# The last block's MLP output products in three rounds instead of two

## The chip, the cores and the metric

The kernel runs on one core of a Trainium2 chip. Its engines work side by side, each through its own instructions in order: PE (TensorE, matrix products), DVE (VectorE), ACT (ScalarE), POOL (GpSimd) and SP (SyncE, which issues all transfers here). They meet only at semaphores. The metric is the device time of one execution in microseconds (us).

## What is computed

For x of 2 x 1024 rows of 2048 numbers, a layer norm is followed by a block with attention and an MLP, and that by a mixture of eight low-rank experts; both are added to x. Three lines of the reference matter here, the MLP with its write, and the expert part that comes last:

```python
mlp_out = jax.nn.silu(gate) * up
hidden_states = rat_write(hidden_states, mlp_out, mlp_wod_w, mlp_wab_w, mlp_wab_b, mlp_du_w, mlp_du_b)
x = x + _L0_ffn_ref(_layernorm(x, axis=-1), L0_ffn_A, L0_ffn_B, L0_ffn_Wr, L0_ffn_br)
```

`rat_write` multiplies the MLP's 2048 hidden values of a row with 632 columns of weights: 512 give `out`, 120 give eight `delta_low` and 112 gate values. A product of `delta_low`, soft-plus and exponentials make a gated update of the row's 2048 hidden numbers from them. All of it is fp32.

## The kernel before

The 2048 rows are 16 tiles of 128 rows, four tiles to a block. The kernel has a projection stage, an attention stage and a mixed stage; the change is in the last one, and there in the fourth block, tiles 12 to 15.

A block has 64 steps on PE. Steps 0 to 31 are the products with the MLP's input weights (L1363). Steps 32 to 63 are the products with its output weights (L1375), in two rounds of 16 steps: the first for tiles 0 and 1 of the block, the second for tiles 2 and 3. Each step takes one of 16 slices of the output weights (128 x 632, `m_wod`, 316 KB) and makes, for each of its two tiles, a product of 512 and one of 120 columns into two banks of PSUM. The weights don't stay on the chip: each round reads all 16 slices again, into a ring of five buffers (NW = 5). SP issues the load for the step five ahead when the step at hand is done.

When a round is over, each of its tiles goes through a write (`w`) and an expert part (`e`), spread over the engines:

- low (L1287 PE, L1418 DVE): the eight `delta_low` are transposed; delta (L1293 PE; L1607 to L1621 ACT; L1423 DVE): their product and the soft-plus
- gates, scale, sum (L1428 to L1471 DVE, L1628 ACT): the gated update; x (L1476 DVE): x is added
- stats (L1502 to L1507 DVE); turn (L1263 PE, L1593 ACT) and down (L1321 PE), each in four quarters: the row is transposed and multiplied with the experts' first factor
- router, weigh (L1512 to L1530 DVE, L1653 ACT), lowT (L1328 PE, L1658 ACT), out (L1333 PE, L1537 DVE) four times, store (SP)

The order of all these is written out by hand. Each step of a block has a place (64 for each block, 1 for each step), each part of a tile stands at a base plus a number, and the list is sorted by place:

```python
W_BASE.update({12: 240, 13: 242, 14: 256, 15: 258})
E_BASE = {**W_BASE, 13: 245.5, 15: 261}
```

Every engine walks this one list and issues its own share, so a part that waits holds up all that stands behind it on its engine. A tile's e part begins 8.5 places behind its base, its store stands at 23. The ring that gives banks to turn, lowT and out has two banks (6 and 7) in the blocks and six after the last step.

Of the kernel before, what the change touches and what calls it, by code (L numbers as in the profile page):

```python
# [11 lines left out]
ALU = mybir.AluOpType  # L12
ACT = mybir.ActivationFunctionType
# [88 lines left out]
def program(nc, x, xT, pos, inv_freq, ident_in, causal_in, spread_in,  # L102
# [3 lines left out]
    with ExitStack() as ctx:  # L106
# [992 lines left out]
        W_BASE = {i: 64 * (i // TB) + 48 + 16 * (i % TB) for i in range(NT - TB)}  # L1099
        W_BASE.update({12: 240, 13: 242, 14: 256, 15: 258})  # L1100
        E_BASE = {**W_BASE, 13: 245.5, 15: 261}
        placed = [(40, ("s", 0, "sum", None))]
        placed += [(64 * blk + step, ("m", blk, step, None)) for blk in range(NBLK) for step in range(64)]
        placed += [(64 * blk - (8.5 - k if blk else .5), ("t", blk, "turn", k)) for blk in range(NBLK) for k in range(RD2 * HCH)]
# [57 lines left out]
        for what, i, part, q in order:  # L1162
# [49 lines left out]
        def used_weights(n):  # L1212
            what, i, k = weights[n]
            if what == "w1":
                sp.wait_ge(write_mm, HCH * i + k + 1)
            elif k < 32:
                sp.wait_ge(mlp_mm, 32 * i + k + 1)
            else:
                sp.wait_ge(wod2_mm, wod2_count(i, (k - 32) // MCH, (k - 32) % MCH))

# [35 lines left out]
        def wait_for_emptied(e, *key):  # L1256
            e.wait_ge(one.sem(key), one.emptied(key))
# [9 lines left out]
        def write_pe(what, i, part, q):  # L1267
# [13 lines left out]
            if part == "low":  # L1281
                if what == "a":
                    wait_for_emptied(pe, what, i, "ab")
                else:
                    wait_for_emptied(pe, "d", i // TB, i % TB // 2, 2 * (i % 2) + 1)
# [68 lines left out]
        def mlp_pe(blk, step):  # L1354
            s = weights_needed("m", blk, step)
            if step < 32:
# [9 lines left out]
                return  # L1366
            q2, k = divmod(step - 32, MCH)
            if k == 0:
                for b in range(4):
                    wait_for_bank(pe, "d", blk, q2, b)  # L1370
# [28 lines left out]
        def write_dve(what, i, part, q):  # L1399
# [43 lines left out]
            if part == "scale":  # L1443
                bs = ab_t[:, DR + 2 * NA:ABW].unsqueeze(1).broadcast_to([P, HS, RH])
                if what == "w":
                    wait_for_emptied(dve, "d", i // TB, i % TB // 2, 2 * (i % 2))
                else:
                    wait_for_emptied(dve, what, i, "out")
# [101 lines left out]
        def mlp_dve(blk, step):  # L1550
            if step < 32:
                g2, mc = UNITS[step]
                if g2 == 1:
                    dve.wait_ge(mlp_mm, 32 * blk + step + 1)
                    wait_for_emptied(dve, "m", blk, step - 2)
                    dve.wait_ge(wod2_mm, 34 * blk)
                    if blk == 0:
# [5 lines left out]
                return  # L1563
            q2, k = divmod(step - 32, MCH)
            if k == MCH - 1:
                for e in range(2):
                    q = 2 * q2 + e
                    dve.wait_ge(wod2_mm, wod2_count(blk, q2, k, e))
                    dve.wait_ge(low_mm, nth("low", "w", (blk - 1) * TB + q) if blk else nth("low", "a", q))
                    V.tensor_tensor(ab2[q][:, :], ps[:, 2 * e + 1, 0:ABW], gates_b[1][:, :],  # L1570
                                    ALU.add).then_inc(emptied[2 * e + 1], 1)

# [22 lines left out]
        def write_act(what, i, part, q):  # L1595
# [8 lines left out]
            if part == "delta":  # L1604
# [64 lines left out]
        def mlp_act(blk, step):  # L1669
            if step < 32:  # L1670
# [235 lines left out]
```

## Time and profile before

| | us |
|---|---|
| median of 3 runs | 1874.6 (1873.32 to 1875.7) |
| the profiled execution's time | 1875.35 |
| its span in the profile | 1873.6 |
| PE busy | 1652.1 (88%) |
| DVE busy | 1171.3 (63%) |
| ACT busy | 794.4 (42%) |
| transfers | 348.69 MB |

The busy shares are means over three stages. The change moves work only in the last 130 us of the span, from the end of the fourth block's first round of output products, and that stretch is to be read by itself. A start in the rows below is in us from the span's start.

### The profile page before, as it was taken

What the parts mean: (1) busy time and instruction counts of PE and PEld (TensorE: products, weight loads), DVE (VectorE), ACT (ScalarE), POOL (GpSimd) and SP (SyncE); (2) the same over time, 40 slices, a digit from 0 to 9 for tenths busy, and PEclk for the clock granted to TensorE, in tenths of its full rate; (3) what the DMA queues carried; (4) which work ended last, traced back from release to release, by engine and by line L of the source; (5) the groups of instructions that cost most, each with busy time, mean ns of one, the idle gap of its engine ahead of it and who ended that gap; (6) DMA issues with size and microseconds to landing.
All of it is one profiled execution on the core that took longest, in us unless ns stands there. A gap on an engine that the chain in (4) does not pass through costs nothing.

```text
span 1873.6 us, 23597 instructions
## 1 busy us (share of the span) xinstructions
PE 1652.1 (88%) x8854; PEld 1141.1 (61%) x8854; DVE 1171.3 (63%) x1873; ACT 794.4 (42%) x1486; POOL 268.7 (14%) x243
## 2 busy tenths in 40 slices
PE   6799998799999956799898999887999998999866
PEld 5565655466666635677565677555677565775544
DVE  6678754688888847344347548547458455555576
ACT  1333235588888725344323444223444322341221
POOL 1235432423340000200002000003000002000000
PEclk7899999899999976699898999998999999999987
DMA  7367568588885152476464665554566544655711
GB/s 298 114 262 254 199 172 238 153 214 238 224 231 125 49 208 90 150 243 215 155 201 155 218 219 199 177 177 149 185 230 212 191 164 148 223 194 172 253 76 68
DMA packets 117221, 348.69 MB, mean 186 GB/s; under 512 B 16226, under 2 KB 33250, under 8 KB 101876
## 3 DMA queue, kind: packets, MB, share of 16 engines
q1 hardware_dynamic: 117108, 347.19, 57.3%
q8 instruction: 70, 1.15, 0.3%
q14 instruction: 43, 0.35, 0.1%
HBM read 271.37 MB, written 75.76 MB: 185 GB/s over the span
## 4 chain that ended last, share of the span: by engine, by line
PE 62%; DVE 22%; ACT 5%; issue 5%; DMA 3%; SPq 2%; POOL 1%; DVEq 0%; ACTq 0%; POOLq 0%
PE ps L1363 15%; PE ps L1375 11%; PE ps L396 4%; PE ps L818 4%; PE ps L1278 4%; PE ps L841 4%; PE ps L805 4%; PE ps L1321 3%; PE ps L1263 3%; PE ps L1306 3%; PE ps L1333 2%; ACT a_p L920 2%; SPq L141 2%; DVE m_A L1436 2%; PE ps L369 2%
## 5 line engine op out<-in xcount | busy, mean ns | idle before, releaser
L1363 PE MATMUL ps<-m_yhi,m_win 128*128 128x512 f32 x1024 | 352.8, 413 | 0.8 <-DMA m_win<-mlp_in_split 0.8
L1375 PE MATMUL ps<-m_wod,m_hT 128*128 128x512 f32 (+1 forms) x1024 | 308.6, 450 | 8.0 <-DVE m_hT L1561 8.0
L1375 PEld LDWEIGHTS ps<-m_wod,m_hT 128*128 128x128 f32 x1024 | 171.8, 199 | 150.1 <-issue 149.7
L1363 PEld LDWEIGHTS ps<-m_yhi,m_win 128*128 128x128 f32 x1024 | 195.4, 191 | 50.1 <-issue 4.9
L862 DVE TENSOR_REDUCE a_negmax<-ps 128x1 f32<-128x640 f32 (+7 forms) x176 | 180.7, 1027 | 63.5 <-PE ps L808 62.7
L920 ACT ACTIVATE a_p<-ps,a_negmax 128x128 f32<-128x128 f32 (+7 forms) x256 | 188.8, 751 | 43.1 <-DVE a_negmax L862 41.0
L1363 PE MATMUL ps<-m_ylo,m_win 128*128 128x512 f32 x512 | 204.0, 398 | 0.0
L818 PE MATMUL ps<-ident,a_p 128*128 128x128 f32 x1152 | 157.9, 276 | 16.1 <-DVE a_pT L875 15.9
L1593 ACT ACTIVATE m_turned<-ps 128x512 f32<-128x512 f32 x128 | 74.1, 593 | 190.2 <-PE ps L1263 190.2
L805 PE MATMUL ps<-a_k,a_q 128*128 128x512 f32 (+3 forms) x384 | 124.5, 403 | 16.6 <-ACT a_p L920 14.7
L818 PEld LDWEIGHTS ps<-ident,a_p 128*128 128x128 f32 x1152 | 123.8, 142 | 18.2 <-DVE a_pT L875 16.8
L1363 PEld LDWEIGHTS ps<-m_ylo,m_win 128*128 128x128 f32 x512 | 98.1, 192 | 24.8 <-issue 4.9
L396 PE MATMUL ps<-p_yT,p_wqkv 128*128 128x512 f32 x256 | 112.3, 593 | 0.0
L1263 PE MATMUL ps<-ident,m_hs 128*128 128x128 f32 x464 | 75.4, 296 | 38.9 <-DVE m_hs L1471 14.0
L1561 DVE TENSOR_TENSOR m_hT<-m_raw,ps 128x512 f32<-128x512 f32 x64 | 43.4, 685 | 106.0 <-PE ps L1363 106.0
L875 DVE COPY a_pT<-ps 128x512 f32<-128x512 f32 (+3 forms) x190 | 108.0, 576 | 0.5
L1708 POOL TENSOR_TENSOR m_scale<-m_scale,mhalf 128x2 f32<-128x2 f32 x16 | 12.4, 774 | 629.3 <-DVE m_scale L1489 629.3
L934 ACT ACTIVATE a_pT<-ps 128x512 f32<-128x512 f32 (+3 forms) x154 | 84.1, 547 | 35.9 <-PE ps L818 35.8
L805 PEld LDWEIGHTS ps<-a_k,a_q 128*128 128x128 f32 x384 | 63.4, 192 | 55.2 <-ACT a_p L920 32.2
L1333 PE MATMUL ps<-e_B,e_lowT 128*128 128x512 f32 x128 | 71.1, 668 | 22.9 <-DVE m_hs L1537 22.2
L1263 PEld LDWEIGHTS ps<-ident,m_hs 128*128 128x128 f32 x464 | 60.1, 155 | 50.5 <-DVE m_hs L1471 15.9
L1679 ACT ACTIVATE m_raw<-ps 128x512 f32<-128x512 f32 x64 | 38.2, 598 | 120.7 <-PE ps L1363 99.0
(202 smaller groups left out, 2737.7 us busy)
## 6 DMA issues: line engine op xcount, KB each, us to landing
m_win<-mlp_in_split SPq DMA_DIRECT2D x128, 512.0 KB, 4.3
m_wod<-in_wod2T SPq DMA_DIRECT2D x128, 316.0 KB, 3.1
m_wod<-in_wod1T SPq DMA_DIRECT2D x64, 316.0 KB, 3.1
p_xT<-in_xT SPq DMA_DIRECT2D x16, 1024.0 KB, 8.9
p_x<-in_x SPq DMA_DIRECT2D x16, 1024.0 KB, 10.4
a_q<-qk_split SPq DMA_DIRECT2D x64, 256.0 KB, 6.5
a_k<-qk_split SPq DMA_DIRECT2D x128, 128.0 KB, 7.1
mlp_in_split<-a_w_two SPq DMA_DIRECT2D x32, 512.0 KB, 3.4
```

The lines of the kernel that those rows point to most:

```text
L396: m = nc.tensor.matmul(ps[:, b, :], wq[:, k, col:col + P], yT[:, k, :], start=(ic == 0), stop=(ic == HCH - 1))
L805: nc.tensor.matmul(ps[:, bank + at, c0:c0 + kn], qs[s][:, qt * P:qt * P + P], ks[s][:, k0:k0 + kn], start=True, stop=k0 + kn < klen)
L818: m = nc.tensor.transpose(ps[:, b, P * m_:P * m_ + P], src[:, j, P * k:P * k + P], ident[:, :])
L841: m = nc.tensor.matmul(ps[32 * hh:32 * hh + 32, 6, c0:P * qn], a_v[s][:, k, HD * hh:HD * hh + HD], kept[:, hh, k, c0:P * qn], start=(k == ...
L862: V.tensor_reduce(negmax[:, n % 4, 0:len(units[n][3])], by_head(n, score_banks(n)), AX_X, ALU.max, negate=True).then_inc(max_ready, 1)
L875: V.tensor_copy(kept[:, heads[j0]:heads[j1] + 1, k0:k1 + 1, P * q:P * q + P], ps[:, b, 0:P * len(part)].rearrange("p (a k b) -> p a k b", ...
L920: m = S.activation(dst[:, j, :], src[:, j, :], ACT.Exp, bias=negmax[:, n % 4, j:j + 1], accum_out=rsum[:, si % 2, q * 4 + hh:q * 4 + hh + 1])
L934: S.activation(kept[:, heads[j0]:heads[j1] + 1, k0:k1 + 1, P * q:P * q + P], ps[:, b, 0:P * len(part)].rearrange("p (a k b) -> p a k b", a ...
L1263: m = nc.tensor.transpose(bank_of(what, i, "turn", q)[:, P * j:P * j + P], h[:, P * (4 * q + j):P * (4 * q + j) + P], ident[:, :])
L1333: nc.tensor.matmul(bank_of("e", i, "out", q), lT[i % 2][:, :], wB[:, 512 * q:512 * q + 512], start=True, stop=True).then_inc(eout_mm, 1)
L1363: m = nc.tensor.matmul(bank_of("m", blk, step), win[s][:, wl, ic, :], y[:, k, :], start=(ic == 0 and p3 == 0), stop=(ic == HCH - 1 and p3 ...
L1375: m = nc.tensor.matmul(ps[:, b, 0:cn], hT[:, k, P * q:P * q + P], w2[s][:, c0:c0 + cn], start=(k == 0), stop=(k == MCH - 1))
```

## The change

In the fourth block the output products go in three rounds: tiles 12 and 13 together as before, then tile 14 alone, then tile 15 alone. The block has 80 steps instead of 64. A step of the two new rounds has two products instead of four, and reads a slice of 316 KB as every step does, so the third reading adds 16 transfers, 5.2 MB.

The parts of tile 14 keep their places (base 256), and those of tile 15 move by 14 for the write (258 to 272) and by 13 for the expert part (261 to 274). Tile 14's banks are 0 and 1 and tile 15's 2 and 3, as before. The ring of banks for the last parts has four (6, 7, 0, 1) after the last step instead of six.

```diff
-        W_BASE.update({12: 240, 13: 242, 14: 256, 15: 258})
-        E_BASE = {**W_BASE, 13: 245.5, 15: 261}
+        W_BASE.update({12: 240, 13: 242, 14: 256, 15: 272})
+        E_BASE = {**W_BASE, 13: 245.5, 15: 274}
+
+        ROUNDS = [[(0, 1), (2, 3)]] * (NBLK - 1) + [[(0, 1), (2,), (3,)]]
...
-        placed += [(64 * blk + step, ("m", blk, step, None)) for blk in range(NBLK) for step in range(64)]
+        placed += [(64 * blk + step, ("m", blk, step, None)) for blk in range(NBLK)
+                   for step in range(32 + MCH * len(ROUNDS[blk]))]
...
-                for b in range(4):
-                    one.plan(("d", i, (part - 32) // MCH, b), b)
-            if what == "m" and (i, part) == (NBLK - 1, 63):
-                one.banks = [6, 7, 0, 1, 2, 3]
+                for q2 in ROUNDS[i][(part - 32) // MCH]:
+                    for b in (2 * (q2 % 2), 2 * (q2 % 2) + 1):
+                        one.plan(("d", i, q2, b % 2), b)
+            if what == "m" and (i, part) == (NBLK - 1, 79):
+                one.banks = [6, 7, 0, 1]
...
-            for e in range(2):
-                q = 2 * q2 + e
-                for c0, cn, b in ((0, H, 2 * e), (H, ABW, 2 * e + 1)):
-                    m = nc.tensor.matmul(ps[:, b, 0:cn], hT[:, k, P * q:P * q + P], w2[s][:, c0:c0 + cn],
-                                         start=(k == 0), stop=(k == MCH - 1))
-                if e == 1 or k == MCH - 1:
+            for q in tiles:
+                for c0, cn, b in ((0, H, 0), (H, ABW, 1)):
+                    m = nc.tensor.matmul(bank_of("d", blk, q, b)[:, 0:cn], hT[:, k, P * q:P * q + P],
+                                         w2[s][:, c0:c0 + cn], start=(k == 0), stop=(k == MCH - 1))
+                if q == tiles[-1] or k == MCH - 1:
                     m.then_inc(wod2_mm, 1)
```

The rest of the diff gives each wait the count that belongs to the new rounds, and lets the copies behind a round go over the round's tiles.

How the list changes the order is seen at two places. The first is PE around the turn of tile 14 (`m_hs_165` is tile 14's hidden row, `e_lowT_200` belongs to tile 13's expert product, `m_wod` to an output product). Before, no output product is left at this point:

```order
L1328 MATMUL ps<-ident,e_weighted_142 128x128
L1333 MATMUL ps<-e_B,e_lowT_200 128x512 x2
L1263 MATMUL ps<-ident,m_hs_165 128x128 x8
L1333 MATMUL ps<-e_B,e_lowT_200 128x512 x2
L1321 MATMUL ps<-e_A,m_turned_188 128x136 x4
L1263 MATMUL ps<-ident,m_hs_165 128x128 x4
```

In the changed kernel the same chain of parts has tile 15's steps between them; shown are steps 9 to 12 of its 16:

```order
L1340 MATMUL ps<-ident,e_weighted_142 128x128
L1388 MATMUL ps<-m_wod_137,m_hT 128x512
L1388 MATMUL ps<-m_wod_137,m_hT 128x120
L1345 MATMUL ps<-e_B,e_lowT_200 128x512
L1388 MATMUL ps<-m_wod_129,m_hT 128x512
L1388 MATMUL ps<-m_wod_129,m_hT 128x120
L1345 MATMUL ps<-e_B,e_lowT_200 128x512
L1275 MATMUL ps<-ident,m_hs_165 128x128 x8
L1388 MATMUL ps<-m_wod_131,m_hT 128x512
L1388 MATMUL ps<-m_wod_131,m_hT 128x120
L1345 MATMUL ps<-e_B,e_lowT_200 128x512 x2
L1388 MATMUL ps<-m_wod_133,m_hT 128x512
```

Seven of tile 15's steps (9 to 15) now stand behind tile 13's weighted values, and five of them (11 to 15) behind the turn of tile 14.

The second place is DVE behind tile 14's sum (the first row of each). Before, tile 15's gates (`m_gate_181`, lane 0) follow at once, and then tile 13's router weights and tile 15's scale:

```order
L1471 TENSOR_TENSOR m_hs_165<-m_hs_165,m_A_168 128x512x3
L1428 TENSOR_TENSOR m_delta_177<-m_delta_177,m_tmp_179 128x512
L1430 SCALAR_TENSOR_TENSOR m_gate_181<-m_mlp_ab_176,m_gate_181 128x48
L1436 TENSOR_TENSOR m_A_167<-m_delta_177,m_gate_181 128x1536
L1437 TENSOR_SCALAR m_gate_181<-m_gate_181 128x48
L1439 RECIPROCAL m_gate_181<-m_gate_181 128x48
L1441 TENSOR_TENSOR m_gate_181<-m_gate_181,m_mlp_ab_176 128x48
L1525 RECIPROCAL e_moments_155<-e_moments_155 128x1
```

In the changed kernel tile 13's router weights, tile 14's x and stats and tile 13's four out additions come first:

```order
L1484 TENSOR_TENSOR m_hs_165<-m_hs_165,m_A_168 128x512x3
L1538 RECIPROCAL e_moments_155<-e_moments_155 128x1
L1540 TENSOR_SCALAR e_router_198<-e_router_198,e_moments_155 128x8
L1543 SCALAR_TENSOR_TENSOR e_weighted_142<-e_low_196,e_moments_155,e_router_198 128x128
L1489 TENSOR_TENSOR m_hs_165<-m_hs_165,m_x 128x2048
L1515 BN_STATS e_stats_152<-m_hs_165 128x6 x4
L1517 BN_AGGR e_moments_156<-e_stats_152 128x2
L1519 TENSOR_SCALAR e_moments_156<-e_moments_156 128x1
L1520 TENSOR_SCALAR e_moments_156<-e_moments_156 128x1
L1550 TENSOR_TENSOR m_last_hs_218<-ps,m_last_hs_218 128x512 x4
L1583 TENSOR_TENSOR m_mlp_ab_176<-ps,m_gate_bias_146 128x120
L1525 SCALAR_TENSOR_TENSOR e_low_150<-e_Asum,e_moments_156,ps 128x136
```

Tile 15's first DVE instruction (L1583, which reads the finished products of its round) moved from ahead of tile 14's gates to behind tile 14's stats.

## Rows read from the trace of the kernel before

**Rows 1.** Busy time of each engine by stretch of 10 us, end of the span
```profile
core 0: us, PE busy (x) PEld busy (x) DVE busy (x) ACT busy (x) POOL busy (x), PEclk, DMA share, GB/s
1770.00:1780.00 10.00, 3.36 (x14) 1.74 (x12) 9.76 (x12) 1.48 (x1) 0.00 (x0) 0.91 0.94 349
...
1820.00:1830.00 10.00, 0.41 (x1) 0.18 (x1) 9.70 (x14) 1.48 (x1) 0.00 (x0) 0.50 0.18 74
```

**Rows 2.** Timeline of PE: start, duration, line, operation [idle before <- releaser]
```profile
1746.21 2.32 PE L1375 MATMUL ps<-m_wod,m_hT 128*128 128x512 f32 x8
1748.37 1.03 PE L1293 MATMUL ps<-m_duT,m_lowT 128*128 128x512 f32 x2
...
1756.79 1.89 PE L1333 MATMUL ps<-e_B,e_lowT 128*128 128x512 f32 x4
...
1781.32 1.97 PE L1263 MATMUL ps<-ident,m_hs 128*128 128x128 f32 x8 [7.96 <-DVE m_hs L1476]
1783.08 5.47 PE L1375 MATMUL ps<-m_wod,m_hT 128*128 128x512 f32 x16
...
1795.45 1.10 PE L1321 MATMUL ps<-e_A,m_turned 128*128 128x136 f32 x8
1796.38 2.32 PE L1375 MATMUL ps<-m_wod,m_hT 128*128 128x512 f32 x8
1798.54 1.10 PE L1321 MATMUL ps<-e_A,m_turned 128*128 128x136 f32 x8
1799.47 1.04 PE L1263 MATMUL ps<-ident,m_last_hs 128*128 128x128 f32 x8
```

**Rows 3.** Timeline of DVE in the same stretch and after it
```profile
1757.85 0.69 DVE L1537 TENSOR_TENSOR m_hs<-ps,m_hs 128x512 f32<-128x512 f32 x1 [1.70 <-PE ps L1333]
...
1773.10 0.68 DVE L1428 TENSOR_TENSOR m_delta<-m_delta,m_tmp 128x512 f32<-128x512 f32 x1
...
1778.98 2.28 DVE L1476 TENSOR_TENSOR m_hs<-m_hs,m_x 128x2048 f32<-128x2048 f32 x1
...
1796.22 0.14 DVE L1507 TENSOR_SCALAR e_moments<-e_moments 128x1 f32<-128x1 f32 x1
...
1809.32 0.68 DVE L1537 TENSOR_TENSOR m_hs<-ps,m_hs 128x512 f32<-128x512 f32 x1
...
1825.23 0.68 DVE L1428 TENSOR_TENSOR m_delta<-m_delta,m_tmp 128x512 f32<-128x512 f32 x1
```

**Rows 4.** Timeline of DVE: weighted values, one tile's statistics, a router
```profile
1828.69 0.16 DVE L1525 RECIPROCAL e_moments<-e_moments 128x1 f32<-128x1 f32 x1
...
1829.45 0.69 DVE L1449 TENSOR_TENSOR m_tmp<-m_delta,m_mlp_ab 128x512 f32<-128x512 f32 x1
...
1841.01 2.46 DVE L1502 BATCH_NORM_STATS2 e_stats<-m_hs 128x6 f32<-128x512 f32 x4
...
1843.94 1.28 DVE L1537 TENSOR_TENSOR m_last_hs<-ps,m_last_hs 128x512 f32<-128x512 f32 x2
...
1851.46 0.34 DVE L1512 SCALAR_TENSOR_TENSOR e_low<-e_Asum,e_moments,ps 128x136 f32<-128x136 f32 x1
...
1853.43 0.35 DVE L1530 SCALAR_TENSOR_TENSOR e_weighted<-e_low,e_moments,e_router 128x128 f32<-128x128 f32 x1
```

**Rows 5.** Timeline of ACT: a soft-plus, first and last instruction
```profile
1749.43 0.60 ACT L1607 ACTIVATE m_tmp<-ps 128x512 f32<-128x512 f32 x1 [4.23 <-PE ps L1293]
...
1751.79 0.24 ACT L1621 ACTIVATE m_gate<-m_gate 128x48 f32<-128x48 f32 x1
```

**Rows 6.** Timeline of PE at the end of the span
```profile
1862.32 0.33 PE L1328 MATMUL ps<-ident,e_weighted 128*128 128x128 f32 x1 [1.71 <-DVE e_weighted L1530]
1863.02 5.40 PE L1333 MATMUL ps<-e_B,e_lowT 128*128 128x512 f32 x8 [0.37 <-ACT e_lowT L1658]
```

**Rows 7.** Issue to landing of the output weights' transfers, 1740 to 1800 us
```profile
DMA to landing us min/median/max: 2.8/3.3/5.5
```

**Rows 8.** Busy time by stretch, a stretch of 2 us
```profile
1720.00:1722.00 2.00, 2.00 (x9) 1.15 (x8) 1.97 (x2) 0.00 (x0) 0.00 (x0) 1.00 1.00 423
```

More of the change, by code:

```diff
@@ L1197, in up_step, with wod2_done @@
             return UNITS.index((1, mc))
-        def wod2_count(blk, q2, k, e=1):
-            return 17 * (2 * blk + q2) + k + 1 + (1 if k == MCH - 1 and e == 1 else 0)
+        wod2_count, wod2_steps = {}, 0
+        for blk in range(NBLK):
+            for r, tiles in enumerate(ROUNDS[blk]):
+                for k in range(MCH):
+                    for q in tiles[-1:] if k < MCH - 1 else tiles:
+                        wod2_steps += 1
+                        wod2_count[blk, r, k, q] = wod2_steps
+        def wod2_done(blk, r, k):
+            return wod2_count[blk, r, k, ROUNDS[blk][r][-1]]
         weights = []
@@ L1218, in used_weights @@
             else:
-                sp.wait_ge(wod2_mm, wod2_count(i, (k - 32) // MCH, (k - 32) % MCH))
+                sp.wait_ge(wod2_mm, wod2_done(i, *divmod(k - 32, MCH)))
         def load_weights(n):
@@ L1284, in write_pe @@
                 else:
-                    wait_for_emptied(pe, "d", i // TB, i % TB // 2, 2 * (i % 2) + 1)
+                    wait_for_emptied(pe, "d", i // TB, i % TB, 1)
                 wait_for_bank(pe, what, i, "low")
@@ L1366, in mlp_pe @@
                 return
-            q2, k = divmod(step - 32, MCH)
+            r, k = divmod(step - 32, MCH)
+            tiles = ROUNDS[blk][r]
             if k == 0:
-                for b in range(4):
-                    wait_for_bank(pe, "d", blk, q2, b)
+                for q in tiles:
+                    wait_for_bank(pe, "d", blk, q, 0)
+                    wait_for_bank(pe, "d", blk, q, 1)
             wait_for_emptied(pe, "m", blk, up_step(k))
-            for e in range(2):
-                q = 2 * q2 + e
-                for c0, cn, b in ((0, H, 2 * e), (H, ABW, 2 * e + 1)):
-                    m = nc.tensor.matmul(ps[:, b, 0:cn], hT[:, k, P * q:P * q + P], w2[s][:, c0:c0 + cn],
-                                         start=(k == 0), stop=(k == MCH - 1))
-                if e == 1 or k == MCH - 1:
+            for q in tiles:
+                for c0, cn, b in ((0, H, 0), (H, ABW, 1)):
+                    m = nc.tensor.matmul(bank_of("d", blk, q, b)[:, 0:cn], hT[:, k, P * q:P * q + P],
+                                         w2[s][:, c0:c0 + cn], start=(k == 0), stop=(k == MCH - 1))
+                if q == tiles[-1] or k == MCH - 1:
                     m.then_inc(wod2_mm, 1)
@@ L1445, in write_dve @@
                 if what == "w":
-                    wait_for_emptied(dve, "d", i // TB, i % TB // 2, 2 * (i % 2))
+                    wait_for_emptied(dve, "d", i // TB, i % TB, 0)
                 else:
@@ L1555, in mlp_dve @@
                     wait_for_emptied(dve, "m", blk, step - 2)
-                    dve.wait_ge(wod2_mm, 34 * blk)
+                    if blk:
+                        dve.wait_ge(wod2_mm, wod2_done(blk - 1, 1, MCH - 1))
                     if blk == 0:
@@ L1563, in mlp_dve @@
                 return
-            q2, k = divmod(step - 32, MCH)
+            r, k = divmod(step - 32, MCH)
             if k == MCH - 1:
-                for e in range(2):
-                    q = 2 * q2 + e
-                    dve.wait_ge(wod2_mm, wod2_count(blk, q2, k, e))
+                for q in ROUNDS[blk][r]:
+                    dve.wait_ge(wod2_mm, wod2_count[blk, r, k, q])
                     dve.wait_ge(low_mm, nth("low", "w", (blk - 1) * TB + q) if blk else nth("low", "a", q))
-                    V.tensor_tensor(ab2[q][:, :], ps[:, 2 * e + 1, 0:ABW], gates_b[1][:, :],
-                                    ALU.add).then_inc(emptied[2 * e + 1], 1)
+                    V.tensor_tensor(ab2[q][:, :], bank_of("d", blk, q, 1)[:, 0:ABW], gates_b[1][:, :],
+                                    ALU.add).then_inc(one.sem(("d", blk, q, 1)), 1)
         def mix_dve():
@@ L1614, in write_act @@
                 else:
-                    wait_for_emptied(act, "d", i // TB, i % TB // 2, 2 * (i % 2) + 1)
+                    wait_for_emptied(act, "d", i // TB, i % TB, 1)
                 act.wait_ge(hs_ready, nth_before("sum", what, i))
@@ L1682, in mlp_act @@
                 return
-            q2, k = divmod(step - 32, MCH)
+            r, k = divmod(step - 32, MCH)
             if k == MCH - 1:
-                for e in range(2):
-                    q = 2 * q2 + e
-                    act.wait_ge(wod2_mm, wod2_count(blk, q2, k, e))
+                for q in ROUNDS[blk][r]:
+                    act.wait_ge(wod2_mm, wod2_count[blk, r, k, q])
                     act.wait_ge(hs_ready, nth("sum", "w", (blk - 1) * TB + q) if blk else nth("sum", "a", q))
-                    S.activation(outs2[q][:, :], ps[:, 2 * e, :], ACT.Copy).then_inc(emptied[2 * e], 1)
+                    S.activation(outs2[q][:, :], bank_of("d", blk, q, 0), ACT.Copy).then_inc(
+                        one.sem(("d", blk, q, 0)), 1)
         def mix_act():
```

## The prediction, made before the changed kernel ran

> **What bounds the kernel now.** I read three views in this order. First the busy time by stretch: in the last 100 us DVE is the full engine, with 9.7 to 9.8 us of 10 in stretches in which PE has 0.4 to 3.4 [rows 1]. So the products are not what sets the end there; DVE's work on one tile's write and expert part is, together with the chain that leads to its start. Second, the timelines of PE and DVE side by side: PE stops 7.96 us for DVE's x of tile 12 before it turns that tile [rows 2], and DVE's tasks stand without a gap from 1757.85 to 1796.36 (38.5 us) and again from 1809.32 on [rows 3]. Between the two DVE has a hole of 13 us, in which PE finishes tiles 14 and 15. That hole, and PE's stop, are what a change of rounds can fill. Third, the end: from the last weighted values, transposed at 1862.32, to the span's end at 1873.6 it is 11.3 us, products, additions and the last store [rows 6].
>
> The change adds no product. It makes tile 14 ready earlier and tile 15 later, and puts steps of tile 15 behind waits for DVE. I therefore follow the new list from about 1744, where the second round begins and up to which the order is the same.
>
> **Part 1, tile 14's first five steps: 5.4 us gained.** A step of two tiles takes 2.16 us (1746.21 to 1748.37) [rows 2], so one of one tile takes 1.08. Ahead of tile 11's out product at 1756.79 [rows 2] stand five steps in both kernels: it moves 5 x 1.08 = 5.4 earlier, to 1751.4, and DVE's addition behind it from 1757.85 to 1752.4. The soft-plus of tile 13 takes 2.6 us on ACT [rows 5] and is over by 1752.9, when DVE still has the addition to do, so nothing else ends late. DVE's block of 38.5 us has the same instructions in the same order [rows 3]: it now ends at 1790.9, and tile 12's x, before at 1781.3, at 1775.9. PE does steps 5 to 10 meanwhile and stops for x from about 1762, 14 us instead of 8.
>
> **Part 2, tile 14 is ready, 7.9 us gained.** After tile 12's turn PE has five steps, downs and turns. By the rows before that took from 1781.32 to 1798.54 [rows 2]; with half the steps and the low clock at its start I get 1775.9 to 1788.2. But DVE takes tile 14's products only behind tile 13's statistics, at 1790.9 to 1791.2. From there PE has to pass, before tile 12's first out addition: low 0.1, four steps of tile 15 (4.3), three downs at 0.93 (1795.45 to 1796.38, so 2.8) [rows 2], delta 0.9 (1.03 long, overlapping what follows) [rows 2], two turns and a lowT (1.0, from 1.04 for two quarters) [rows 2]. That is 9.1, and 1.06 to the addition (1756.79 to 1757.85 [rows 2, 3]): 1801.4, where it was 1809.32 [rows 3].
>
> **Part 3, tile 14's gates to stats.** DVE's block from that addition to tile 14's sum is the same list, 1809.32 to 1825.23, 15.9 us [rows 3]: it ends at 1817.3. Then come tile 13's weighted values (0.8) [rows 4], tile 14's x (2.2) and its statistics, 1841.01 to 1843.94, 2.9 [rows 4]: 1823.2. Up to here the changed kernel is ahead.
>
> **Part 4, tile 15's last seven steps, where the gain is lost.** PE ends step 8 of tile 15 at about 1809.1 and then finds the transpose of tile 13's weighted values in its queue, which come at 1818.1: 9 us of idle PE. Then it has the transpose and its copy (0.4), steps 9 and 10 and two out products (3.9 at the upper clock, some 6.3 with the restart at the lower), two quarters of tile 14's turn, which share two banks with these outs and wait for DVE's additions behind the statistics (1.3), and then steps 11 to 15 (5.4), two outs (1.75), three downs (2.8) and two turns (0.9). Sum: 1818.1 + 0.4 + 6.3 + 1.3 + 10.9 = 1837.0. Before, tile 15's products were complete at 1798.5 [rows 2]; they are 38 us later, and DVE, which has nothing but four additions after 1823.2, waits for them.
>
> **Part 5, tile 15 alone.** From 1837.0: the last down 0.93 (it stands ahead of low), low, router and copy 1.1, delta 0.95, soft-plus 2.6 [rows 5], ACT's copy of tile 14's transposed values 0.3, the out product and its addition 1.06: DVE goes on at 1844.0. One tile's gates, scale and sum with its neighbour's outs took 1757.85 to 1773.10, 15.25 us [rows 3], and x 2.3 [rows 3]: 1861.5. In the kernel before, all of this work of tile 15 was laid between tile 14's, with DVE full [rows 1]. Then PE alone: two quarters turned at the lower clock 1.97 [rows 2], four downs 3.7, two turns 0.9, and about 1.1 for what of the downs falls to the lower clock: 7.7. From the router's first instruction to the end of the weighted values 2.3 (1851.46 to 1853.78) [rows 4], and the 11.3 from there to the end [rows 6]. Sum: 1861.5 + 7.7 + 2.3 + 11.3 = 1882.8.
>
> **The sum.** The span goes from 1873.6 to 1882.8, +9.2. The profiled execution's time is 1875.35, 1.75 above its span and 0.75 above the median of three; I add the 9.2 to the median: 1883.8 us, 0.5% slower.
>
> **Costs with two bounds.** *The clock.* After a stop PE restarts at the lower of its levels: 8 transposes took 1.97 us after the stop of 7.96, and 1.04 without one; two steps of two tiles right behind took 5.47 where one takes 2.32 [rows 2], so 4.5 for two; 1820 to 1830 shows a granted clock of 0.50 (the 1.2 GHz level) with PE idle [rows 1]. I carry 2.4 us for this in part 4, 2.0 in part 5 and 1.8 in the last eight products, whose eight records took 5.40 [rows 6] where four at the upper level took 1.89 [rows 2]. With none of it the sum is 1876.6; with the lower level in part 5's first products too, +1.5, it is 1884.3. The nearest row is the restart at 1781.32, which paid, so I keep the middle value. The Trainium skill says as much (TensorE: Matmul & The Clock Gate, "Loop structure matters more than you think"): products with long waits between them run at the lower clock, which here speaks against the change, since it makes the stop at tile 12 longer and adds one at tile 13. By this rule, the trace agrees.
>
> *The third reading of the weights.* A step needs 316 KB in 1.08 us, 300 GB/s, twice the rate of before. A slice lands 2.8 to 5.5 us after its issue, 3.3 in the middle [rows 7], and five buffers leave four steps, 4.3 us, between the issue and the use. At 3.3 it costs nothing; at 5.5 each step takes 5.5 / 4 = 1.38, 0.3 more. Only steps on the path pay: five in part 1 had their loads issued in the slow first round, four in part 2 while PE stopped, and the five of part 4 too, since their loads are issued by 1819. I take 0, and 1.5 as the upper bound (five steps), nothing below 0, since a transfer can't hasten a step. The engines moved 423 GB/s in a stretch of 2 us [rows 8], so 300 is within reach.
>
> The Trainium skill gives a limit of about 358 GB/s for one core's HBM traffic (DMA: Bandwidth & Descriptors, "Specifications"). The 423 GB/s in a row of this case is above it, so the row decides. By the page a slice would take 0.9 us, an estimate from its figure, still less than a step, and the sum would stay.
>
> *The ring of banks.* Two banks instead of six for the last parts of tile 13 and 14: 0.9 us of the 1.3 above at part 4. The least is 0, the most two DVE additions, 1.4.
>
> **Rivals.**
> *A, the overlap works.* PE gets tile 15's products done while DVE is on tile 14, in the 9 us that it has free, and DVE goes from tile 13's out additions at 1825.7 straight on to tile 15's gates: 1825.7 + 15.25 + 2.3 = 1843.3, + 21.3 = 1864.6, so 1865.6 us, 9 faster. It decides at tile 15's last step: by 1818.7 it is A, later it is not. For it speaks PE's room; against it, the order, which has seven of the steps behind values that come at 1818.1. 6%.
> *B, about the same.* The two gains hold and the clock stays up nearly everywhere: span 1876.6, 1877.6 us. Against it is the restart at 1781.32 [rows 2]. 10%.
> *C, the weights come late as well.* Slices land late beside the 1 MB loads and stores, in part 2 and part 4, some nine steps at 0.3 and one stop of 2 for a slice behind such a store: + 4.7, 1888.5. For it speaks the share of 0.94 at 349 GB/s in 1770 to 1780, when slices and two 1 MB loads go together [rows 1]. 12%.
> *D, the change doesn't do what it says* (the products of tile 14 not complete before those of tile 15): excluded, the new order on PE shows both rounds apart.
> The forecast, 1879.5 to 1886.5, has the other 72%.
>
> **How the numbers follow.** What a measurement of this kernel can tell from no change is about 0.2%, 3.7 us. Faster is A, 6%. Same is B and the lowest edge of the forecast, 10%. Slower is the rest of the forecast and C, 84%. The range leaves out A and the edges of B and C: 1878.0 to 1889.0.
>
> **What would show it.** In the changed kernel's profile: DVE's addition to tile 11's row at about 1752.4 and tile 14's sum ending near 1817 (parts 1 to 3); PE idle some 14 us before 1776 and 9 us before 1818 on DVE's x and weighted values (part 4); tile 15's bias addition (L1583) near 1837; a hole of more than 10 us on DVE between 1829 and 1844; tile 15's x at 1861. If that bias addition comes before 1820, A holds. If PE's waits for slices (on the transfers of the weights) are above 2 us in total, C. If the clock reads 1.0 from 1818 to 1826 and at the last turn, B. What would make the prediction wrong is a wait that I have put in the wrong place in part 4, since each us there goes to the end undiminished.

## The result and the profile after

The changed kernel takes 1884.5 us (median of 4 runs, 1883.8 to 1887.0), the kernel before on the same chip 1875.2 (1873.3 to 1875.8). The ratio is 1.0054, with a 95% interval from 1.0037 to 1.0071: slower by 0.5%. The interval belongs to the record's ratio over all runs; the quotient of the two medians is 1.0050. Forecast were 1883.8 and a range from 1878.0 to 1889.0.

The profiled execution has a span of 1885.2 us, 11.6 more than before. The second round begins 1.0 us later in it (VectorE's addition of the bias for tile 12 at 1742.95, before at 1741.94), and up to there both kernels have the same order, so that microsecond isn't the change's. From this addition to the end it is 142.25 us, before 131.66: **+10.6**. The kernels are compared below by this tail and by their medians. A tail is that of one execution, here the slowest of the four, and the medians differ by 9.4.

The busy page tells little: the sums hardly move (PE 1652.1 to 1658.3 us, DVE 1171.3 to 1172.2), and the extra transfers (353.87 MB, 5.2 more) are the only plain sign of the change.

```profile
DMA packets 119525, 353.87 MB, mean 188 GB/s; under 512 B 16482, under 2 KB 33506, under 8 KB 104180
```

The timelines tell it. First PE in the changed kernel (start, duration, line, operation, idle before and who ended it); L1388 are the output products, `x4` is one step of one tile:

```profile
1749.56 0.30 PE L1340 MATMUL ps<-ident,e_weighted 128*128 128x128 f32 x1 [0.32 <-DVE m_delta L1436]
...
1777.24 1.97 PE L1275 MATMUL ps<-ident,m_hs 128*128 128x128 f32 x8 [13.21 <-DVE m_hs L1489]
1779.00 4.20 PE L1388 MATMUL ps<-m_wod,m_hT 128*128 128x512 f32 x8
...
1819.93 0.48 PE L1340 MATMUL ps<-ident,e_weighted 128*128 128x128 f32 x1 [8.73 <-DVE e_weighted L1543]
1820.20 2.33 PE L1388 MATMUL ps<-m_wod,m_hT 128*128 128x512 f32 x4
...
1826.78 0.66 PE L1275 MATMUL ps<-ident,m_hs 128*128 128x128 f32 x4 [0.28 <-DVE m_last_hs L1550]
1827.27 1.24 PE L1388 MATMUL ps<-m_wod,m_hT 128*128 128x512 f32 x4
...
1836.98 1.24 PE L1388 MATMUL ps<-m_wod,m_hT 128*128 128x512 f32 x4
...
1844.23 5.38 PE L1345 MATMUL ps<-e_B,e_lowT 128*128 128x512 f32 x8 [2.57 <-ACT e_lowT L1671]
1864.01 1.97 PE L1275 MATMUL ps<-ident,m_last_hs 128*128 128x128 f32 x8 [14.40 <-DVE m_last_hs L1489]
...
1874.68 5.40 PE L1345 MATMUL ps<-e_B,e_lowT 128*128 128x512 f32 x8 [0.37 <-ACT e_lowT L1671]
```

PE stops 13.21 us for tile 12's x (before 7.96 [rows 2]), then 8.73 us for tile 13's weighted values with steps 9 to 15 of tile 15 queued behind them. The first of these steps runs at 1820.20, the last at 1836.98. The kernel before had ended its last step before 1799 [rows 2].

The same on DVE; L1583 is its first instruction of a tile's write, L1489 the addition of x:

```profile
1753.78 0.69 DVE L1550 TENSOR_TENSOR m_hs<-ps,m_hs 128x512 f32<-128x512 f32 x1 [0.62 <-PE ps L1345]
...
1792.20 0.27 DVE L1583 TENSOR_TENSOR m_mlp_ab<-ps,m_gate_bias 128x120 f32<-128x120 f32 x1
...
1803.11 0.69 DVE L1550 TENSOR_TENSOR m_hs<-ps,m_hs 128x512 f32<-128x512 f32 x1 [5.79 <-PE ps L1345]
...
1819.07 0.15 DVE L1538 RECIPROCAL e_moments<-e_moments 128x1 f32<-128x1 f32 x1
...
1829.42 0.69 DVE L1550 TENSOR_TENSOR m_last_hs<-ps,m_last_hs 128x512 f32<-128x512 f32 x1 [2.69 <-PE ps L1345]
...
1838.25 0.28 DVE L1583 TENSOR_TENSOR m_mlp_ab<-ps,m_gate_bias 128x120 f32<-128x120 f32 x1 [7.28 <-PE ps L1388]
...
1846.34 0.69 DVE L1550 TENSOR_TENSOR m_hs<-ps,m_hs 128x512 f32<-128x512 f32 x1 [3.61 <-PE ps L1345]
...
1861.66 2.29 DVE L1489 TENSOR_TENSOR m_last_hs<-m_last_hs,m_last_x 128x2048 f32<-128x2048 f32 x1
```

Tile 12's out addition is 6.2 us earlier than before (1803.11 against 1809.32 [rows 3]), 7.2 counted from each tail's start. From 1831.0 to 1838.25 DVE has nothing. Tile 15's x starts at 1861.66; in the kernel before it starts at 1845.13:

```profile
1845.13 2.28 DVE L1476 TENSOR_TENSOR m_last_hs<-m_last_hs,m_last_x 128x2048 f32<-128x2048 f32 x1
```

By stretch (columns as in [rows 1]) DVE's hole is plain: it is busy 6.89 and 1.82 us of 10. The changed kernel:

```profile
1820.00:1830.00 10.00, 9.72 (x29) 5.05 (x30) 6.89 (x11) 1.47 (x3) 0.54 (x1) 0.81 0.24 66
1830.00:1840.00 10.00, 9.26 (x58) 6.97 (x56) 1.82 (x7) 1.79 (x3) 0.00 (x0) 1.00 0.82 308
```

The kernel before, with DVE busy 9.86 us of 10 (for 1820 to 1830 see [rows 1]):

```profile
1830.00:1840.00 10.00, 8.55 (x25) 4.73 (x24) 9.86 (x8) 1.47 (x3) 0.00 (x0) 0.69 0.00 0
```

PE never waits for a slice of the weights. Its waits from 1740 us on are all for DVE and ACT (the four longest are shown: us in total, times, longest), and the slices land in 2.6 to 6.6 us, 3.1 in the middle (before [rows 7]):

```profile
PE ps L1275 <- DVE m_last_hs L1489: 14.4, 1, 14.4
PE ps L1275 <- DVE m_hs L1489: 13.2, 1, 13.2
PE ps L1340 <- DVE e_weighted L1543: 10.9, 2, 8.7
PE ps L1345 <- ACT e_lowT L1671: 2.9, 2, 2.6
```

### The profile page after: what moved, and what is told of

Same layout as the page of the kernel before. It is cut to its first block, busy times and chain, and to the rows that moved or that the text cites. A ratio compares the mean times of both kernels' runs of the same rounds, so it can differ in the third digit from the quotient of the medians.

```text
span 1885.2 us, 23613 instructions
## 1 busy us (share of the span) xinstructions
PE 1658.3 (88%) x8854; PEld 1144.3 (61%) x8854; DVE 1172.2 (62%) x1873; ACT 794.5 (42%) x1486; POOL 268.4 (14%) x243
## 2 busy tenths in 40 slices
DMA packets 119525, 353.87 MB, mean 188 GB/s; under 512 B 16482, under 2 KB 33506, under 8 KB 104180
## 4 chain that ended last, share of the span: by engine, by line
PE 65%; DVE 21%; ACT 5%; issue 4%; DMA 2%; SPq 1%; POOL 1%; DVEq 0%; ACTq 0%; POOLq 0%
PE ps L1375 15%; PE ps L1388 11%; PE ps L396 6%; PE ps L818 4%; PE ps L1290 4%; PE ps L841 4%; PE ps L805 4%; PE ps L1333 3%; PE ps L1275 3%; PE ps L1318 3%; PE ps L1345 3%; PE ps L369 2%; ACT a_p L920 2%; DVE m_A L1449 2%; DVE m_A L1480 2%
## 5 line engine op out<-in xcount | busy, mean ns | idle before, releaser
L1388 PE MATMUL ps<-m_wod,m_hT 128*128 128x512 f32 (+1 forms) x1024 | 317.2, 457 | 8.0 <-DVE m_hT L1575 8.0
L1388 PEld LDWEIGHTS ps<-m_wod,m_hT 128*128 128x128 f32 x1024 | 177.0, 203 | 155.8 <-issue 155.6
## 6 DMA issues: line engine op xcount, KB each, us to landing
p_x<-in_x SPq DMA_DIRECT2D x16, 1024.0 KB, 10.6
```

Of the source, the lines that this page charges most:

```text
L1388: m = nc.tensor.matmul(bank_of("d", blk, q, b)[:, 0:cn], hT[:, k, P * q:P * q + P], w2[s][:, c0:c0 + cn], start=(k == 0), stop=(k == MCH - 1))
```

## The experiments

The theory (order): tile 15's last seven steps stand in PE's queue behind values that DVE delivers late, and by then DVE has no other work, so tile 15's write lies alone at the end. The rivals are the third reading of the weights and the clock. Ratios are to the kernel before, measured on the same chip beside it (the median of the kernel before was 1873.1 to 1873.5 beside e1 to e8), and differ by up to 0.001 from the quotient of the medians. Each experiment has ten runs, e3 and the changed kernel four. The changed kernel wasn't run again beside e1 to e4; e3, which makes the same products there, gives its median, 1884.5. The tail runs from tile 12's bias addition to the end of the span.

| kernel | median us | ratio (95%) | tail us |
|---|---|---|---|
| before | 1875.2 | 1 | 131.66 |
| changed | 1884.5 | 1.0054 (1.0037 to 1.0071) | 142.25 |
| e1 steps early | 1878.4 | 1.0022 (1.0011 to 1.0033) | 137.99 |
| e2 and tile 15 early | 1870.9 | 0.9980 (0.9969 to 0.9990) | 128.53 |
| e3 small loads | 1884.5 | 1.0050 (1.0031 to 1.0070) | 142.18 |
| e4 fill | 1880.5 | 1.0037 (1.0027 to 1.0046) | 139.06 |
| e5 gates first | 1870.9 | 0.9989 (0.9979 to 1.0000) | 130.89 |
| e6 gates and fill | 1871.7 | 0.9989 (0.9980 to 0.9999) | 130.99 |
| e7 before, filled | 1872.9 | 0.9999 (0.9990 to 1.0009) | 131.13 |
| e8 before, places | 1875.6 | 1.0012 (1.0003 to 1.0022) | 134.49 |

### e1: the steps out of DVE's shadow

The changed kernel with tile 15's steps 7 to 15 ahead of tile 13's weighted values in the list; all parts of the tiles stay in place.

```diff
-        placed += [(64 * blk + step, ("m", blk, step, None)) for blk in range(NBLK)
-                   for step in range(32 + MCH * len(ROUNDS[blk]))]
+        placed += [(262.1 + 0.08 * (step - 71) if step >= 71 else 64 * blk + step, ("m", blk, step, None))
+                   for blk in range(NBLK) for step in range(32 + MCH * len(ROUNDS[blk]))]
```

> Only the places of tile 15's steps 7 to 15 change: 262.1 to 262.74, one behind the other, ahead of the transpose of tile 13's weighted values, into the 8.7 us in which PE stood idle. All parts of tiles 12 to 15 keep their places. Theory O (the loss is the order: seven steps stand behind waits for DVE, five of them behind the turn of tile 14): those five steps, 5.4 us, leave the path between the turn and tile 15's low, so the time falls from 1884.5 by some 5.4, to 1879; DVE's waits for products of tile 15 go. Rival W (slices of the weights come late, the third reading costs the time): nine steps in a row at 1.08 us ask for 300 GB/s for 10 us, PE would stop for slices, and the time stays at 1884 or rises. Rival K (the loss is the restart of PE's clock): about as before, 1883 to 1884.5, since the stops stay.

Measured: 1878.4 us, 1.0022, so 6 us of the changed kernel's loss are gone. PE now does the nine steps in one run, and its stop for the weighted values is 0.99 instead of 8.73:

```profile
1805.58 10.05 PE L1388 MATMUL ps<-m_wod,m_hT 128*128 128x512 f32 x36
1816.62 0.33 PE L1340 MATMUL ps<-ident,e_weighted 128*128 128x128 f32 x1 [0.99 <-DVE e_weighted L1543]
```

DVE takes tile 15's products at 1816.48, but its low, delta and gates still stand behind tile 14's last down. It idles 4.89 us ahead of tile 14's router values and 3.61 us ahead of the addition that precedes tile 15's gates:

```profile
1816.48 0.28 DVE L1583 TENSOR_TENSOR m_mlp_ab<-ps,m_gate_bias 128x120 f32<-128x120 f32 x1
...
1830.97 0.35 DVE L1525 SCALAR_TENSOR_TENSOR e_low<-e_Asum,e_moments,ps 128x136 f32<-128x136 f32 x1 [4.89 <-PE ps L1333]
...
1838.12 0.69 DVE L1550 TENSOR_TENSOR m_hs<-ps,m_hs 128x512 f32<-128x512 f32 x1 [3.61 <-PE ps L1345]
```

So the seven steps carry 6 us by the medians and 4.3 by the tails of the two profiled executions (142.25 to 137.99). What is left over the kernel before, 4 us by the ratio and 6.3 by the tail, is for the second half of the theory.

### e2: and tile 15's write beside tile 14's expert part

e1, and tile 15's parts at 264.4 and 267.5.

```diff
-        W_BASE.update({12: 240, 13: 242, 14: 256, 15: 272})
-        E_BASE = {**W_BASE, 13: 245.5, 15: 274}
+        W_BASE.update({12: 240, 13: 242, 14: 256, 15: 264.4})
+        E_BASE = {**W_BASE, 13: 245.5, 15: 267.5}
```

> As e1_steps_early, and tile 15's parts stand earlier too (base 264.4 for the write, 267.5 for the expert part, instead of 272 and 274), so that its delta and gates follow tile 14's stats on DVE at once. Theory O: this is the overlap that rival A of the prediction described; DVE is full from tile 14's gates to tile 15's stats, and the time falls below the kernel before, to 1866 to 1870. Rival W: 1880 or more. If only splitting as such cost time (two more stops, half-size steps), it would stay above 1875.

Measured: 1870.9 us, 0.9980 (0.9969 to 0.9990), faster than both kernels, though 1 us above the upper end of what was expected. Order alone wins the whole loss back. In DVE's timeline tile 15's x now starts at 1842.67, 101.2 us into the tail instead of 118.7, and its gate work covers tile 14's turns and downs; the price is PE's stop of 10.8 us before tile 14's lowT:

```profile
1818.28 0.28 DVE L1583 TENSOR_TENSOR m_mlp_ab<-ps,m_gate_bias 128x120 f32<-128x120 f32 x1
...
1842.67 2.29 DVE L1489 TENSOR_TENSOR m_last_hs<-m_last_hs,m_last_x 128x2048 f32<-128x2048 f32 x1
```

```profile
1845.75 0.47 PE L1340 MATMUL ps<-ident,e_weighted 128*128 128x128 f32 x1 [10.80 <-DVE e_weighted L1543]
```

### e3: a quarter of the bytes in the third reading

The third round's transfers bring 158 of the 632 columns (79 KB instead of 316); in the other columns tile 15's products are made with an earlier slice's numbers.

```diff
-                move(w2[s][:, :], wod2T[(k - 32) % MCH]).then_inc(wt_loaded[s], 16)
+                if k < 64:
+                    move(w2[s][:, :], wod2T[(k - 32) % MCH]).then_inc(wt_loaded[s], 16)
+                else:
+                    move(w2[s][:, 0:158], wod2T[(k - 32) % MCH][:, 0:158]).then_inc(wt_loaded[s], 16)
```

> The changed kernel, in which the third round's transfers of weights read 158 of 632 columns (79 KB instead of 316 KB); the other columns keep what the buffer held, so tile 15's numbers are not the reference's. Number and order of transfers and of all waits are the same. Theory O: the third reading is hidden, within 1 us of the changed kernel, 1884. Rival W: the bandwidth of the third reading is on the path, 2 to 5 us faster.

Measured: 1884.5 us, the tail 142.18 against 142.25. The transfers land in 1.9 us instead of 3.1, and nobody was waiting for them. The first row is e3's, from 1775 to 1840, the second the changed kernel's, from 1740 to 1845 (over e3's stretch its middle value is 2.9):

```profile
DMA to landing us min/median/max: 1.8/1.9/3.9
```

```profile
DMA to landing us min/median/max: 2.6/3.1/6.6
```

So three quarters of the third reading's bytes cost nothing, and with no wait of PE for a slice (above) rival C falls.

### e4: PE's stops filled

Products that nobody reads, 128x512 into a bank out of use, in four of PE's stops. They keep the granted clock up; nothing of the kernel's own work is changed.

```diff
+        def fill(n):
+            for _ in range(n):
+                nc.tensor.matmul(ps[:, 4, :], ident[:, :], wB[:, 0:512], start=True, stop=True)
+
         def expert_pe(i, part, q):
+            if part == "turn" and q == 0 and i in (12, 15):
+                pe.wait_ge(eB_loaded, 32)
+                fill(14 if i == 12 else 16)
+            if part == "lowT" and i == 13:
+                fill(9)
+            if part == "out" and q == 0 and i == 14:
+                fill(2)
```

> The changed kernel with products that nobody reads (128x512, into PSUM bank 4, 0.87 us each) laid in PE's stops: 14 ahead of tile 12's turn, 9 ahead of the transpose of tile 13's weighted values, 2 ahead of tile 14's out products, 16 ahead of tile 15's turn. They keep PE's clock at its upper level over the stops. My prediction carried 6.2 us for the clock. If that is right: 4 to 6 us faster, 1879 to 1880.5, with the turn of tile 15 at 1.04 instead of 1.97 us. If the low clock lies beside waits for DVE: under 2 us. A fill that is too long would show as PE starting tile 12's or tile 15's turn later than DVE's x.

Measured: 1880.5 us, 4.0 less by the medians, the low edge of what was expected; by the tail and by the ratios it is 3.2, less than expected. The trace tells why (L1344 is the down, L1356 the out product, L1399 an output step):

```profile
1773.05 1.09 PE L1275 MATMUL ps<-ident,m_hs 128*128 128x128 f32 x8 [1.21 <-DVE m_hs L1500]
1773.98 2.32 PE L1399 MATMUL ps<-m_wod,m_hT 128*128 128x512 f32 x8
...
1788.35 0.27 PE L1299 MATMUL ps<-ident,m_mlp_ab 128*8 128x128 f32 x1 [1.08 <-DVE m_mlp_ab L1594]
...
1821.41 1.16 PE L1275 MATMUL ps<-ident,m_hs 128*128 128x128 f32 x8 [1.73 <-DVE m_last_hs L1561]
...
1839.38 3.70 PE L1356 MATMUL ps<-e_B,e_lowT 128*128 128x512 f32 x8 [0.86 <-ACT e_lowT L1682]
1858.24 1.09 PE L1275 MATMUL ps<-ident,m_last_hs 128*128 128x128 f32 x8 [1.43 <-DVE m_last_hs L1500]
```

The eight transposes and two steps take 3.1 us (1773.05 to 1776.14) instead of 5.8, 2.7 less, but PE then waits for DVE, 1.08 us of it for the bias addition of tile 14, and tile 12's out addition comes only 0.3 us earlier in the tail (59.90 against 60.16 us after its beginning). Behind tile 13's weighted values the wait for DVE's out additions grows from 0.28 to 1.73 us, and tile 15's bias addition is in all 0.65 earlier (94.65 against 95.30). Only where DVE has nothing to do but wait for PE does the clock go to the end: 0.9 us at the out products of tile 14 and 1.6 at the last turns and downs. Sum: 0.3 + 0.4 + 0.9 + 1.6 = 3.2.

### e5 and e6: can more be had?

e5 is e2 with tile 14's write moved a tenth of a place, so that its gates stand on DVE ahead of tile 12's out additions, in the hole of 5.79 us. e6 is e5 with 14 fill products ahead of tile 12's turn and 10 ahead of tile 14's lowT.

```diff
-        W_BASE.update({12: 240, 13: 242, 14: 256, 15: 264.4})
-        E_BASE = {**W_BASE, 13: 245.5, 15: 267.5}
+        W_BASE.update({12: 240, 13: 242, 14: 255.9, 15: 264.4})
+        E_BASE = {**W_BASE, 13: 245.5, 14: 256, 15: 267.5}
```

> The kernel with tile 15's nine steps early and tile 15's MLP ahead of tile 14's low, and besides: tile 14's delta and gates stand on VectorE ahead of tile 12's additions of out, into which that kernel's VectorE runs 5.79 us too early and waits for TensorE. Same work, other order. Theory order (what the change costs is the order of one queue behind another, and work moved into a hole of a queue comes off the end): from 1791 us on VectorE has work without a break of note up to the last tile, so of the 5.79 us the delta product, the gate instructions and the 1.76 us m_A product move in (about 3.3 us), and the time is 1870.9 - 3 = 1868 us, 0.995 to 0.998 of the kernel before. Theory clock (the low granted clock and what TensorE does late sets the last tiles): VectorE's hole is not on the path, 1870 to 1872. If tile 12's additions, now later, hold their banks so that TensorE stops before tile 15's steps: over 1872.

> The kernel with the gates first, and 14 products that nobody reads in TensorE's stop ahead of tile 12's turn (13.2 us there), 10 in its stop ahead of tile 14's lowT product (10.8 us), each 128x512 into an unused bank; they add work and no result. Theory order alone: the turn of tile 12 at the upper level takes 1.1 instead of 2.0 us and the first steps behind it 2.1 instead of 4.1, in all at most 3 us, of which VectorE, which has work of its own there, passes on about none in the middle and about 1.4 us at tile 14's out product: 1866 to 1868. Theory clock: 4 us and more, under 1865. If the filling holds up the turn: slower than the kernel with the gates first alone.

Measured: 1870.9 us (0.9989) and 1871.7 (0.9989): neither gains on e2. Both expectations failed: the 3 us of e5 and the further 1.4 of e6 aren't there. In e5 the work did move into the hole, but another hole opens ahead of tile 15's bias addition, since PE has completed the steps by then and no sooner:

```profile
1797.57 0.69 DVE L1441 TENSOR_TENSOR m_delta<-m_delta,m_tmp 128x512 f32<-128x512 f32 x1 [0.70 <-ACT m_tmp L1624]
...
1802.72 1.48 DVE L1550 TENSOR_TENSOR m_hs<-ps,m_hs 128x512 f32<-128x512 f32 x2 [1.71 <-PE ps L1345]
...
1818.11 0.28 DVE L1583 TENSOR_TENSOR m_mlp_ab<-ps,m_gate_bias 128x120 f32<-128x120 f32 x1 [1.89 <-PE ps L1388]
```

In e2 both queues came to this point together (DVE at 1818.28 without a wait); e5 relieves only one of them. The theory of order predicted a gain because I had followed DVE's queue alone. e6 shortens tile 12's turn from 1.97 to 1.09 us as well, and that too ends in waits (2.59 us for DVE's bias addition of tile 14).

### e7: does the kernel before pay for the clock?

The kernel before with 8 fill products ahead of tile 12's turn, 18 ahead of tile 13's lowT and 5 ahead of the third quarter of tile 14's turn.

```diff
+            if part == "turn" and (i, q) == (12, 0):
+                pe.wait_ge(eB_loaded, 32)
+                fill(8)
+            if part == "lowT" and i == 13:
+                fill(18)
+            if part == "turn" and (i, q) == (14, 2):
+                fill(5)
```

> The kernel before with products that nobody reads: 8 in TensorE's stop of 8.0 us ahead of tile 12's turn, 18 ahead of tile 13's lowT product, 5 ahead of the third quarter of tile 14's turn. Asks whether the clock's price, 3 to 4 us in the changed kernel, is one that the change brings. If the change brings it (the longer stop of 13.2 us and the lone tile 15): the kernel before gains 0 to 1 us, 1872.5 to 1873.5. If the old order pays it as well: 2 to 4 us faster, 1869 to 1871, and what the clock adds to the change's cost is near nothing.

Measured: 0.9999 (0.9990 to 1.0009), no gain, the tail 0.5 us shorter. Tile 15's x does start 1.75 us earlier in the tail (1841.81 in a tail begun at 1740.37, against 1845.13 and 1741.94), but then the addition of tile 14's out waits 4.81 us for PE:

```profile
1841.81 2.28 DVE L1487 TENSOR_TENSOR m_last_hs<-m_last_hs,m_last_x 128x2048 f32<-128x2048 f32 x1
...
1855.04 0.69 DVE L1548 TENSOR_TENSOR m_hs<-ps,m_hs 128x512 f32<-128x512 f32 x1 [4.81 <-PE ps L1344]
```

Part of that wait is again the clock. Behind a stop of 2.50 us tile 15's first down, and what follows it, runs at the lower level (the record of the down takes 2.15 us), where the kernel before had no such stop and took 1.19. The row of e7, then that of the kernel before:

```profile
1848.63 2.15 PE L1332 MATMUL ps<-e_A,m_turned 128*128 128x136 f32 x8 [2.50 <-DVE e_low L1523]
```

```profile
1852.21 1.19 PE L1321 MATMUL ps<-e_A,m_turned 128*128 128x136 f32 x8 [0.25 <-ACT m_turned L1593]
```

From this down to the first out product of tile 14 it takes 5.35 us in e7 (1848.63 to 1853.98) and 3.87 before, so the filled kernel loses 1.5 of its gain to a clock that the filling didn't hold. With it held, an estimate from these rows is a tail 2 us shorter than before. So these runs don't show how much of the 3.2 us of e4 is a cost that the change brings: all of it by e7 as measured, some 1.2 (3.2 less 2.0) by the estimate. Between the two filled kernels 7 of the 10 us remain (1.0037 against 0.9999; by the tails 7.9); e1 and e2 show those to be the order.

### e8: the places of e2 without the third round

The kernel before, two rounds, with tile 15's places from e2 (the same two numbers, 264.4 and 267.5).

> The kernel before, two rounds, with only the places of tile 15 moved to those of the second experiment (write 258 to 264.4, expert part 261 to 267.5), so that tile 14's x, statistics and turn stand ahead of tile 15's gates and scale. The question is where the second experiment's gain of 3 to 4 us over the kernel before is from. If from the places alone: about 1870 to 1871 here too. If from the round of its own, which makes tile 14 complete earlier and starts VectorE's work on it 7.7 us earlier (the addition of out at 1801.6 where it was 1809.3): nothing is gained here. The last tile's chain behind its x then has no neighbour's work beside it, as in the second experiment, and the sum is VectorE's block of tile 15 ending as late as before (1851) plus the lone turns, downs and router: 1873 to 1879, most likely 1876.

Measured: 1875.6 us, 1.0012 (1.0003 to 1.0022), as expected. The places alone lose a little (0.1%, by the tail 2.8 us); e2's gain needs the round of its own. Tile 12's out addition stands at 1806.53 here, 66.1 us into the tail, and in e2 at 1801.60, 60.1 into its own. Tile 15's x is at 105.2 here (1845.62) and at 101.2 there: of the 6.0 us that the round gives at the first place, 4.0 are left at the second. The tails differ by 6.0 again, but 1.7 of that is the clock at the last out products (3.70 us in e2, 5.40 in e8), which is no merit of the round (see the last section).

## Why the prediction was right

The forecast was slower by 9.2 us and the medians differ by 9.4. That these agree to 0.2 is in part luck: in the profiled pair the tail grew by 10.6, 1.4 more than the sum, and in part 4 errors of opposite sign cancel. The path is the one that was forecast; the prediction's times with the 1.0 us by which this execution's second round starts late, against the trace:

| | forecast + 1.0 | trace |
|---|---|---|
| tile 11's out addition | 1753.4 | 1753.78 |
| tile 12's x ended, PE turns | 1776.9 | 1777.24 |
| DVE takes tile 14 | 1791.9 | 1792.20 |
| tile 12's out addition | 1802.4 | 1803.11 |
| tile 14's sum ended | 1818.3 | 1819.07 |
| DVE takes tile 15 | 1838.0 | 1838.25 |
| DVE goes on with tile 15 | 1845.0 | 1846.34 |
| tile 15's x ended | 1862.5 | 1863.95 |
| end of the span | 1883.8 | 1885.2 |

**Parts 1 and 2** hold within 0.4 us up to tile 14's start. The 0.4 at tile 11's out addition is a wait that the sum had at nothing: PE stopped 0.32 for DVE's delta of tile 12 (1749.56). Tile 12's out addition came 0.7 late. Of that 0.3 was there when DVE took tile 14, and e4 shows another 0.3 to be the low clock behind tile 12's turn (two one-tile steps took 4.20).

**Part 3** holds: 15.9 us of DVE's block, 15.96 measured (1803.11 to 1819.07).

**Part 4** is right in its sum and not in its terms. I carried 2.4 us for the clock and 1.3 for the two banks as if they added up. In the trace PE waits only 0.28 for a bank; e4, with the clock up, waits 1.73 there. It is the same time paid once, and the clock's own share is 0.4 (of the 0.65 that e4 gained up to tile 15's bias addition, 0.3 were there before). From the weighted values to step 11 it took 7.4 us (1819.87 to 1827.27) instead of the 8.0 of the sum. That the total came out at 1838.25 (forecast 1838.0) is luck: the weighted values themselves were 0.8 late, and the path behind them 0.6 shorter; behind step 11 it took 11.0 us to DVE's addition, where I had 10.9.

**Part 5** is the one that was too small, by 1.1: from DVE's taking of tile 15 to its going on it took 8.1 us, not 7.0. Delta and soft-plus were as forecast (2.0 and 4.0 us against 2.0 and 3.9). The out product at the lower clock took 2.1 us up to its addition, not 1.06. The prediction had named it as an upper bound of 1.5 and carried nothing. Behind it the lone block (17.6 us to the end of x), the turns and downs (7.9), the router (2.1) and the end (11.2) match to 0.2.

**The clock** in all: 6.2 us were carried. e4 removed 3.2: 1.6 of the 2.0 carried at the last turns and downs, 0.4 of part 4's 2.4, and 1.2 at two places where the sum had no term of its own (tile 12's turn and tile 14's out products). At the last out products e4 has no fill and the clock is low (5.27 against 5.40). Their 1.8, by the rows 5.40 - 2 x 1.89 = 1.6, the kernel before pays as well [rows 6]; it is no part of the difference.

**The third reading** at 0: confirmed by e3. **The cause**, seven steps behind the weighted values and tile 15's write with no neighbour: confirmed by e1 (-6 us, by the tail -4.3) and e2 (-14 us in all, 1.0054 to 0.9980). Rival A, the overlap that works, was a true possibility of this very split, with tile 15's steps and parts placed as in e2, and gave 1870.9 rather than its 1865.6. Its tile 15 was 2 us too early at x, and it had 21.3 us from there to the end, where e2 has 25.0 (1844.96 to 1870.0): tile 14's out products, behind PE's stop of 10.8 us, stand ahead of tile 15's turns.

## What to carry to other kernels

Splitting a round to have one tile sooner pays only if the rest of the round isn't queued behind a value of the engine that it should keep fed: read on each in-order engine what the moved instruction stands behind, and when that is delivered. Filling one queue's hole gains only up to the point where the other queue arrives, so follow both to their next meeting point before you count it. A price (a clock, a bank) that is paid while another wait runs is paid once; carry the larger of the two, not the sum.

## What the runs showed of the hardware that I had not expected

The granted clock behind a stop is not a fixed price. In e2 and e5 PE does the same products in the same order from tile 14's lowT on, and stops equally long, 2.19 and 2.18 us, ahead of the last weighted values. The eight records of the out products then take 3.70 us in one and 5.40 in the other:

```profile
1860.43 0.33 PE L1340 MATMUL ps<-ident,e_weighted 128*128 128x128 f32 x1 [2.19 <-DVE e_weighted L1543]
1861.12 3.70 PE L1345 MATMUL ps<-e_B,e_lowT 128*128 128x512 f32 x8 [0.37 <-ACT e_lowT L1671]
```

```profile
1860.90 0.33 PE L1340 MATMUL ps<-ident,e_weighted 128*128 128x128 f32 x1 [2.18 <-DVE e_weighted L1543]
1861.60 5.40 PE L1345 MATMUL ps<-e_B,e_lowT 128*128 128x512 f32 x8 [0.37 <-ACT e_lowT L1671]
```

The granted clock by stretches of 2 us (the first number behind POOL), of e2 and then of e5: the one stays at 1.00, the 2.4 GHz level, the other falls to 0.50, the 1.2 GHz level.

```profile
1862.00:1864.00 2.00, 2.00 (x6) 0.95 (x5) 1.38 (x2) 0.00 (x0) 0.00 (x0) 1.00 0.00 0
1864.00:1866.00 2.00, 0.82 (x2) 0.00 (x0) 1.38 (x2) 0.00 (x0) 0.00 (x0) 1.00 0.00 0
```

```profile
1862.00:1864.00 2.00, 2.00 (x4) 0.71 (x3) 0.69 (x1) 0.00 (x0) 0.00 (x0) 0.69 0.00 0
1864.00:1866.00 2.00, 2.00 (x4) 0.90 (x3) 0.69 (x1) 0.00 (x0) 0.00 (x0) 0.50 0.00 0
```

What decided it these runs don't show. What came earlier was not quite equal: the first six records of tile 14's out products took 4.26 us in e2, with a stop of 0.82 us soon after, and 5.49 in e5, with none. The last out products explain 1.6 of the 2.4 us between these two tails, and are why I don't call e2 better than e5. The Trainium skill (TensorE: Matmul & The Clock Gate, "Loop structure matters more than you think") names the waits between products as the cause of the lower clock. The stops and restarts of this kernel agree (1.97 us for eight transposes behind 13.21 us, 1.09 with the stop filled), but the pair above has the same stop ahead of the last products and both clocks.
